# Rotary 16-wide attention: the norm's rows are turned one round later, behind the scores and ahead of the mixed values, and the key products follow these

## The reference, cut to what matters

```python
    def _L1_attn_ref(X, Wq, Wk, Wv, Wo):
        ...
        Q = apply_rope((X @ Wq).reshape(Bs, Ts, H, dh))
        K = apply_rope((X @ Wk).reshape(Bs, Ts, Hkv, dh))
        V = (X @ Wv).reshape(Bs, Ts, Hkv, dh)
        ...
        scores = jnp.einsum('bkgtd,bksd->bkgts', Qh, Kh) / jnp.sqrt(jnp.float32(dh))
        ...
        attn = jax.nn.softmax(scores, axis=-1)
        out = jnp.einsum('bkgts,bksd->bkgtd', attn, V)
        ...
        return out @ Wo
    ...
    x = _layernorm(x + _L1_attn_ref(x, L1_attn_Wq, L1_attn_Wk, L1_attn_Wv, L1_attn_Wo), axis=-1)
    x = _layernorm(x + _L1_xattn_ref(x, ctx_4096, ctx_4096, mask_BxSxS2_ff0, L1_xattn_wq, L1_xattn_wk, L1_xattn_wv, L1_xattn_wo, 0), axis=-1)
```

## Time and profile before

| what | us |
|---|---|
| median of 3 runs | 2548.92 (2546.95 to 2550.6) |
| the profiled execution, its own time | 2545.74 |
| span of its trace, first to last instruction | 2544.4 |
| PE busy in it | 2432.2 (96%) |
| DVE busy | 1666.3 (65%) |
| ACT busy | 992.8 (39%) |
| the rotary stage, about | 855 to 1044 |

### The profile page before, as it was taken

One profiled execution on the slowest core, in us unless ns is written; L12 is line 12 of the kernel. 1 busy time (PEld: TensorE's weight loads), 2 busy tenths in 40 slices (PEclk: granted clock), 3 DMA queues, 4 the chain that ended last, 5 costly groups with the idle time before them and its releaser, 6 DMA issues.

```text
span 2544.4 us, 36687 instructions
## 1 busy us (share of the span) xinstructions
PE 2432.2 (96%) x12504; PEld 1523.0 (60%) x12504; DVE 1666.3 (65%) x3133; ACT 992.8 (39%) x3612; POOL 734.0 (29%) x755
## 2 busy tenths in 40 slices
PE   8999999999999798999999999998998989999998
PEld 7865666666655565456666666556664554555554
DVE  3477777777765677677777777665665644445565
ACT  0013444434444466343444444523555412323330
POOL 1037344443422111363345433222220221000002
PEclk9999999999999899999999999999999999999999
DMA  8552233222222366121333222322551020224430
GB/s 177 101 145 71 75 104 96 87 79 79 88 87 75 104 199 203 64 83 59 99 95 98 84 74 82 92 92 93 195 186 55 22 75 30 96 70 153 129 100 33
DMA packets 220378, 249.90 MB, mean 98 GB/s; under 512 B 49792, under 2 KB 165952, under 8 KB 218144
## 3 DMA queue, kind: packets, MB, share of 16 engines
q1 hardware_dynamic: 212128, 218.20, 29.1%
q10 hardware_dynamic: 8064, 29.36, 3.0%
HBM read 161.49 MB, written 85.98 MB: 97 GB/s over the span
## 4 chain that ended last, share of the span: by engine, by line
PE 84%; DVE 9%; ACT 2%; DMA 2%; issue 2%; POOL 1%; SPq 0%; DVEq 0%; ACTq 0%; POOLq 0%
PE banks L770 14%; PE banks L858 12%; PE banks L735 4%; PE banks L920 4%; PE banks L751 4%; PE banks L886 4%; PE banks L303 3%; PE banks L842 3%; PE banks L2113 3%; PE banks L1543 3%; PE banks L2164 3%; PE banks L2490 2%; PE banks L2453 2%; PE banks L2141 2%; PE banks L2183 2%
## 5 line engine op out<-in xcount | busy, mean ns | idle before, releaser
L969 ACT ACTIVATE E_x<-S_x,sm_x 128x128 f32<-128x128 f32 x512 | 199.2, 390 | 296.9 <-DVE sm_x L1143 296.9
L1205 POOL TENSOR_TENSOR QT<-QT,const 128x512 f32<-128x512 f32 x128 | 172.2, 1345 | 421.0 <-DVE turned L1023 421.0
L161 POOL TENSOR_TENSOR norm_spread<-norm_mv,const 128x1 f32<-128x1 f32 x96 | 20.9, 217 | 909.8 <-DVE norm_mv L157 909.8
L770 PE MATMUL banks<-xT,weights 128*128 128x512 f32 x512 | 235.2, 593 | 1.8 <-DVE QT L1040 1.8
L2611 ACT ACTIVATE E_s<-banks,top_s 128x128 f32<-128x128 f32 x512 | 180.5, 380 | 95.8 <-DVE top_s L2718 95.8
L1101 DVE TENSOR_TENSOR x<-banks,x 128x256 f32<-128x256 f32 (+1 forms) x288 | 147.1, 511 | 82.9 <-PE banks L858 76.8
L858 PE MATMUL banks<-weights,OT 128*128 128x256 f32 x768 | 194.9, 384 | 5.9 <-DVE weights L1084 5.9
L858 PEld LDWEIGHTS banks<-weights,OT 128*128 128x128 f32 x768 | 143.3, 190 | 68.7 <-issue 28.0
L976 ACT ACTIVATE OT<-banks 128x512 f32<-128x512 f32 x128 | 76.2, 595 | 249.3 <-PE banks L920 249.3
L1207 POOL TENSOR_TENSOR QT<-QT,turned 128x512 f32<-128x512 f32 x128 | 169.2, 1322 | 10.0
L982 ACT ACTIVATE E_x<-E_x,sm_x 128x128 f32<-128x128 f32 x512 | 162.2, 390 | 2.0 <-DVE sm_x L1157 2.0
(11 more groups left out here) (320 smaller groups left out, 4896.9 us busy)
## 6 DMA issues: line engine op xcount, KB each, us to landing
scratch_pt<-blocks_x SPq DMA_DIRECT2D x124, 256.0 KB, 2.0
PT<-scratch_pt SPq DMA_DIRECT2D x496, 64.0 KB, 2.0
scratch_latent_pt<-blocks_s ACTq DMA_DIRECT2D x56, 512.0 KB, 3.7
PT_s<-scratch_latent_pt SPq DMA_DIRECT2D x224, 128.0 KB, 3.0
weights<-in_L_xwq SPq DMA_DIRECT2D x64, 256.0 KB, 3.9
weights<-in_L_xwo SPq DMA_DIRECT2D x64, 256.0 KB, 4.3
scratch_latent_pt<-blocks SPq DMA_DIRECT2D x30, 512.0 KB, 2.6
PT<-scratch_latent_pt SPq DMA_DIRECT2D x120, 128.0 KB, 2.9
```

Source lines behind the costliest of these rows:

```text
L770: mm = PE.matmul(to, left[:, k, head], moving, start=name in ("P1", "P2", "P4", "P5") and k == 0, stop=k == 1, skip_group_check=name in (" ...
L969: ins = AC.activation(head_of(e, j, u), scores_of(s, j, u), ACT.Exp, bias=sm[:, 0, j:j + 1], scale=1.0, accum_out=sm[:, 1, j:j + 1])
L1205: PO.tensor_tensor(four(to), four(to), spread(cos128, 4), ALU.mult).then_inc(*pool_step.one())
```

## The change

In the rounds that come one after a round of `turned_at` (10, 14, 18, 22, 26 and 30), PE now issues the scores, the norm's turn, the mixed values and then the key products, where before the norm's turn stood at the end of the round before, and the key products stood ahead of the mixed values. On ACT the norm's copy moves from the end of the earlier round to the next one, behind the copy of the mixed values. The last turn (block 6) stands behind the loop, where it stood before in effect.

```diff
--- before.py
+++ after.py
@@ -2551,18 +2551,23 @@
                             turn_direct(s - 1)
                         if early(s)[0] == "turn_q":
                             product(early(s)[1], "turn_q")
+                        if rotary and turned_at(s - 1) is not None:
+
+                            if turned_at(s - 1) + 3 < B:
+                                PE.wait_ge(*s_qsin(turned_at(s - 1) + 4))
+                            norm.turn(turned_at(s - 1))
+                            for r in mixes(s):
+                                mix(r)
                         kind, at = late(s)
                         if kind:
                             product(at, kind)
-                        for r in mixes(s):
-                            mix(r)
+                        if not (rotary and turned_at(s - 1) is not None):
+                            for r in mixes(s):
+                                mix(r)
                         if early(s)[0] == "turn_k":
                             product(early(s)[1], "turn_k")
-                        if rotary and turned_at(s) is not None:
-
-                            if turned_at(s) + 3 < B:
-                                PE.wait_ge(*s_qsin(turned_at(s) + 4))
-                            norm.turn(turned_at(s))
+                    if rotary:
+                        norm.turn(turned_at(last - 1))
 
                 def act_small():
                     def raw_copy(b, kind):
@@ -2593,6 +2598,8 @@
                             if r >= 2:
                                 AC.wait_ge(*s_divided(r - 1))
                             AC.activation(mixed[r % 2][:, :, :].rearrange("p a n -> p (a n)"), psum[6][:, 0:2 * P], ACT.Copy).then_inc(*s_mixed_here.one())
+                        if rotary and turned_at(s - 1) is not None:
+                            norm.copy(turned_at(s - 1))
                         if direct < s <= ROUNDS:
                             r = s - 1
                             AC.wait_ge(*s_mix(r - 2))
@@ -2617,9 +2624,8 @@
                         if rotary:
                             if kind == "q":
                                 raw_copy(at, kind)
-                            if turned_at(s) is not None:
-                                norm.copy(turned_at(s))
                     if rotary:
+                        norm.copy(turned_at(last - 1))
                         norm.copy(B - 1)
 
                 def dve_small():
```

## The result

| what | before | changed |
|---|---|---|
| median, us | 2548.92 (7 runs, 2542.48 to 2551.52) | 2562.36 (7 runs, 2556.53 to 2571.01) |
| ratio to before | | 1.0064, 95% interval 1.0049 to 1.0078 |
| span of the profiled execution | 2544.4 | 2569.7 |
| round 8's query product to the stage's last output product | 135.0 | 155.2 |

The change makes the kernel slower: 13.4 us by the medians. The ratio isn't the quotient of these two medians, which is 1.0053; taken by itself it stands for about 16 us, and its interval for 12.5 to 19.9. The forecast was 2561.4, 12.5 slower, in a range of 2552 to 2573.

A forecast was written before the change was run, and what follows sets the result against it. PE was taken to bound the kernel (84% of the chain), with its waits for `turned` being DVE's work. Terms 6.3 + 2.5 + 1.3 + 2.4 gave 12.5 us slower, median 2561.4, range 2552 to 2573.

The forecast's parts named there:

- The sign and its cause: Whole kernel: 12.5 us slower, mainly because the transfer wait then has the key products queued behind it; slower given 0.85.
- The mixed values go ahead of the key products: Rotary stage rounds: key products no longer cover the transfers; in round 22 the key's turn comes 0.85 us later.
- The price of a landing: Rounds with moved mixed values: key's turn at the transfer's landing plus 3.9 us (0.73, 2.05 and 1.1).
- What DVE allows: Five places in the rotary stage: DVE could reach `KT` at most 0.7 us earlier per place, 3.5 in all.
- Rounds 10 and 18: Transfers land late there; key's turn 3.9 instead of 0.73 us after the landing, costing 3.1 each, 6.3 together.
- Rounds 14, 22 and 26 taken alike: All three priced like round 22, 0.85 us each, 2.5 in all; bounds per round 0.7 gain to 3.1 loss.
- PE's clock: Holes of rounds 10 and 18: one fall to 0.50 costing 2.4 us, with none and two as bounds.
- Round 30: Norm's copy on ACT waits for the turn behind E's transposes, so copies start 1.3 us later; at best 0.
- The sum: Whole kernel: 6.3 + 2.5 + 1.3 + 2.4 = 12.5 us slower, 2558.2 profiled and 2561.4 median.
- The cover pays: Rival: transfers have landed in time, five waits for `turned` vanish, 5.4 us faster, 2543.5; chance 0.03.
- DVE's path hides both: Rival: DVE sets the pace, landings come 1 us sooner; 0 to 5 us lost, about 2551; chance 0.12.
- Every place becomes a hole: Rival: five places each cost 3.1 us plus up to 2.4 of clock, 29 in all, 2578; over 23: 0.10.

The follow-up runs named there:

- Experiment 2: Kernel before with only the mixed values moved ahead of the key products, norm's turn and copy unmoved: 2557.44 us against 2545.32 before, ratio 1.0044.
- Experiment 3: Changed kernel, five groups' mixed values made from a tile of zeros, so no transfer waited for: 2546.92 us against 2545.32 before, ratio 1.0003.
- experiment 7: Kernel before with only the norm's turn behind the scores and its copy moved, rounds 10 to 26: 2544.28 us against 2543.89 before, ratio 1.0002.
- experiment 4: Changed kernel, but block 5's turn and copy stay in round 29, round 30 as before: 2559.97 us against 2545.32 before, ratio 1.0058.
- experiment 5: Changed kernel plus 14 dummy matmuls ahead of the mixed values in rounds 10, 18 and 26: 2558.23 us against 2543.89 before, ratio 1.0047.
- experiment 1: Changed kernel, but key products stay ahead of the mixed values, only turn and copy moved: 2546.36 us against 2545.32 before, ratio 1.0006.

## Why the prediction was right, point by point

- **The sign and its cause.** "The mixed values go ahead of the key products" was the step that carried the loss. Experiment 2 does it alone and loses 0.44%. Experiment 3 takes the waiting away and loses nothing.
- **The price of a landing.** The forecast had the key's turn at the landing plus 3.9. Measured at full clock: 3.76 in round 22 of the changed kernel. For round 22 it forecast 0.85, and 0.65 came by the length of the place.
- **What DVE allows.** The forecast bounded the gain by 0.7 a place, against the 1.3 that PE stood idle. Round 14 gained 0.29 in one trace of four, and experiment 7 0.3 to 0.6. The bound held and the gain is about half of it, since the key's turn then waits for ACT's copy of the keys and for `V`.
- **Rounds 10 and 18.** Forecast 3.1 each (3.9 less 0.73 is 3.2). Without the clock the two places lost 2.1 and 2.9 against before (23.09 and 24.11 by the line, against 20.99 and 21.19). One comparison in the forecast is uneven: its 4.3 and 4.5 us after the turn are starts of mixed values, its 1.9 for round 22 is a landing; the mixed values of round 22 started 3.65 after the turn. The sum goes by the landings and isn't hurt. The wait in round 10 was to be 3 us or more and was 2.56.
- **Rounds 14, 22 and 26 taken alike.** This step was wrong for round 26. Its transfer landed late in every trace where the mixed values stand first and the hole isn't filled: they waited 2.74 us for it in the changed kernel, 2.06 when it ran again, 2.59 in experiment 4 and 1.93 in experiment 2. In the trace of before round 26 looked like 22, as its mixed values waited for nothing. But the row of its last transfer was there to be read, as the earlier trace rows was for round 22:

```profile
L2739 SPq DMA_DIRECT2D PT_s<-scratch_latent_pt x1: 433/433/433, 1000.0 to 1000.0; - x1
...
DMA to landing us min/median/max: 3.6/3.6/3.6
```

It landed at 1003.5, 2.7 us after the turn of that place (1000.83), where it was 1.9 in round 22. With the landing plus 3.9 that gives a key's turn at 1007.4 against 1005.79, 1.6 later and not 0.85. Without the clock, round 26 of the changed kernel lost about 2.3.

- **PE's clock.** Forecast: one fall, 2.4 us, with two as the bound. Both traces of the changed kernel have three more than before, in rounds 10, 18 and 26, with about 11 us in the first; the second has a stretch 5.2 us shorter, 150.0. The term was too small by 8.9 us in the first trace, more than the 7.7 by which that stretch missed the forecast. The price of one fall ranged from 1.6 us (3.4 us at 0.50) over 2.2 (6.8) to 5.4 (13.6).
- **Round 30.** Forecast 1.3. Measured 1.29 from the transposes of E to the mixed values (6.35 against 5.06), 1.2 from round 28 to the end (32.4 against 31.2), and about 1 by experiment 4.
- **The sum.** 12.5 forecast, 13.4 by the medians. The profiled execution's stretch lost 20.2, and its terms show what the agreement is worth: the five places without the clock lost 7.7 (forecast 8.8), round 30 lost 1.2 (1.3), the clock 11.3 (2.4). The other trace lost 15.0. The mechanism and the terms of waiting were right, the clock's size was not, and how often each hole brings the clock down in the runs that were not profiled isn't known. So the agreement of the sum to 1 us is partly luck.
- **The rivals.** "The cover pays" fell with the changed kernel itself, and experiment 3 shows that even without the five waits nothing measurable is gained. "DVE's path hides both" describes experiment 3, not the change. "Every place becomes a hole" came half true: three of five. The section HAM oscillation of TensorE: Matmul & The Clock Gate in the Trainium skill, which spoke for this rival, was nearer to what happened than the one fall that the sum held. In the changed kernel's trace the clock fell at and behind three holes, of 2.56, 3.58 and 2.74 us.

Left open: why the landings alternate, late for rounds 10, 18 and 26 and earlier for 14 and 22. In the trace of before, the stores to DRAM for rounds 10 and 18 took 5.3 and 5.2 us from issue to landing and those for 14, 22 and 26 took 3.5 to 3.7; the last transfer back took 4.0 and 4.3 against 3.1, 3.2 and 3.6. What lengthens them wasn't tried, by moving a store or a transfer by itself. Experiment 3 changes two things at once, the wait and the data that the mixed values read; no run keeps the data and takes the wait alone away.

## What to carry to other kernels

Before moving a wait forward on an in-order engine, look up when the thing waited for arrives, also where the profile shows no wait for it: a landing that is covered leaves no trace in the list of waits. Only the transfer's own row shows it, for round 22 and the row at 1000.0 for round 26. An idle stretch of the busiest engine is worth no more than the engine that it waits for can give: five waits of 1.1 us went here and came back as five waits of 1.07. And a hole can be dearer than its length, since PE's clock may fall behind it: in the first trace the 2.56 us of round 10 were followed by a fall that cost 5.4.

## What was not expected of the hardware

- The length of a hole doesn't tell the length of the fall behind it. In round 10, 2.56 us of waiting were followed by 13.6 us at 0.50, and 3.77 us (the changed kernel once more) by 6.8. With 1.7 us of dummy matmuls in a gap of 4.0 us (experiment 5, round 10) the clock stayed at 1.00.
- Nor does its length tell whether there is a fall. A hole of 1.60 us was followed by one (round 22 of experiment 5, where the place took 23.67 us and the line gives 22.1), and so was one of 1.91 (round 10 of experiment 1). Holes of 2.48 us (round 10 of experiment 4) and of 1.89 and 1.93 (rounds 10 and 26 of experiment 2) were not.
- The seven runs of the changed kernel range over 14 us, and the two traces of it differ by 5.2 in the stretch (155.2 and 150.0) and by 11.3 in the span (2569.7 and 2558.4). So more than half of what sets these two executions apart lies outside the stretch that was changed, and a single trace is a poor measure of a change of a few microseconds. The length of one place at full clock, less its lag, repeats to 0.02 us in nine of the ten places at hand.
